# Reordering the transpositions of an attention kernel's output stage

## The reference

```
q, k, v = x @ Wq.T, x @ Wk.T, x @ Wv.T        # 32 heads of 16
q, k    = rope(q), rope(k)
scores  = q k^T / 4 + banded learned bias, causal
attn    = softmax(scores, with a learned offset per head in the denominator) @ v
x1 = layernorm(x + attn @ Wo.T)
y  = mxfp4(x1) @ mxfp4(W).T + b               # blocks of 32 along the row, values rounded to fp4
x2 = layernorm(x1 + y)
```

## Time and profile before

| what | value |
|---|---|
| median of 3 runs | 1728.17 us (1727.54 to 1734.26) |
| the profiled execution's own time | 1727.92 us |
| its span, first to last instruction | 1726.1 us |
| PE busy | 1555.8 us, 90% |
| DVE busy | 1229.9 us, 71% |
| ACT busy | 913.1 us, 53% |
| POOL busy | 194.6 us, 11% |
| mean granted PE clock | 0.952 of full |

### The profile page before, as it was taken

How to read it: one execution, slowest core, us unless ns; L and a number is a source line. 1 busy time by engine, 2 the same in 40 slices (tenths; PEclk the granted TensorE clock), 3 DMA queues, 4 the chain that set the end, 5 groups by cost and what they waited for, 6 DMA issues and landing times.

```text
span 1726.1 us, 59784 instructions
## 1 busy us (share of the span) xinstructions
PE 1555.8 (90%) x22214; PEld 776.2 (45%) x22224; DVE 1229.9 (71%) x3801; ACT 913.1 (53%) x1276; POOL 194.6 (11%) x92
## 2 busy tenths in 40 slices
PE   7999999948998998999899899999999999788773
PEld 3444444412554554555455455455455454344331
DVE  2444444368887888788788788788788884378775
ACT  2333333211665665566566566565566667466764
POOL 4333333240000000000000000000000000023322
PEclk9999999955999999999999999999999999899995
DMA  5444444761343353263264245245244302112211
GB/s 214 148 146 146 158 157 153 137 177 28 79 84 63 70 101 54 59 113 62 53 109 72 53 90 88 56 84 86 63 79 83 70 16 88 37 60 75 73 61 61
DMA packets 127057, 155.70 MB, mean 90 GB/s; under 512 B 18321, under 2 KB 82961, under 8 KB 126514
## 3 DMA queue, kind: packets, MB, share of 16 engines
q1 hardware_dynamic: 126770, 151.86, 37.1%
HBM read 100.52 MB, written 50.50 MB: 87 GB/s over the span
## 4 chain that ended last, share of the span: by engine, by line
PE 60%; DVE 16%; issue 15%; ACT 4%; DMA 2%; POOL 2%; DVEq 1%; SPq 0%; POOLq 0%; ACTq 0%
PE ps L645 14%; PE ps L712 10%; PE ps L671 10%; PE ps L691 10%; PE ps L805 7%; PE ps L697 6%; DVE junk L1152 6%; DVE mx L1145 4%; POOL probs L1024 2%; PE ps L722 1%; DVE mx L1152 1%; ACT probs L947 1%; DMA k_stack<-k_parts 1%; ACT k_stack L937 1%; DMA attn<-wvT 1%
## 5 line engine op out<-in xcount | busy, mean ns | idle before, releaser
L892 ACT ACTIVATE probs<-ps 128x1024 f32<-128x1024 f32 (+3 forms) x768 | 604.2, 812 | 379.9 <-PE ps L697 346.3
L1152 DVE CUSTOM_DVE_ANT_0 junk<-ps,bias_q 128x384 bf16<-128x384 f32 (+2 forms) x1024 | 500.6, 502 | 112.7 <-PE ps L671 92.8
L671 PE MATMUL ps<-k_stack,q_stack 96*32 96x384 bf16 (+3 forms) x6144 | 520.3, 341 | 56.3 <-DVE mx L1152 31.7
L691 PE MATMUL ps<-q_stack,k_stack 99*32 99x512 bf16 (+3 forms) x6144 | 515.1, 333 | 10.0 <-issue 7.7
L1145 DVE TENSOR_REDUCE mx<-ps 128x1 f32<-128x128 f32 (+3 forms) x768 | 362.3, 485 | 34.1 <-PE ps L671 29.3
L697 PE MATMUL ps<-toep,flip 96*32 96x384 bf16 (+2 forms) x5120 | 371.7, 284 | 5.7 <-issue 5.5
L645 PE MATMUL ps<-attn 128*128 128x512 f32 x768 | 332.2, 595 | 10.8 <-DMA attn<-hT 9.6
L712 PE MATMUL ps<-probs,v_sb 128*32 128x512 f32 (+3 forms) x3072 | 318.6, 488 | 0.1
L671 PEld LDWEIGHTS ps<-k_stack,q_stack 96*32 96x32 bf16 x6144 | 169.2, 97 | 297.8 <-DVE mx L1152 106.0
L645 PEld LDWEIGHTS ps<-attn 128*128 128x128 f32 x768 | 146.6, 191 | 195.5 <-issue 195.5
L691 PEld LDWEIGHTS ps<-q_stack,k_stack 99*32 99x32 bf16 x6144 | 167.7, 96 | 137.6 <-issue 68.4
(11 more groups left out here) (98 smaller groups left out, 983.5 us busy)
## 6 DMA issues: line engine op xcount, KB each, us to landing
q_stack<-q_parts SPq DMA_DIRECT2D x192, 128.0 KB, 4.1
k_stack<-k_parts SPq DMA_DIRECT2D x192, 128.0 KB, 4.1
v_dram<-v_sb SPq DMA_DIRECT2D x32, 512.0 KB, 2.7
v_sb<-v_dram SPq DMA_DIRECT2D x128, 128.0 KB, 3.8
q_parts<-q_stack SPq DMA_DIRECT2D x96, 128.0 KB, 1.9
k_parts<-k_stack SPq DMA_DIRECT2D x96, 128.0 KB, 2.0
attn<-hT SPq DMA_DIRECT2D x8, 1024.0 KB, 6.2
q_stack<-h SPq DMA_DIRECT2D x16, 512.0 KB, 4.1
```

The costliest lines, as they stand in the source:

```text
L671: mm = pe.matmul(ps_ring[STRIP * a:STRIP * (a + 1), use.bank, 0:c1 - c0], q_stack[0:STACK, b, hl, i:i + STRIP], k_stack[0:STACK, b, hl, c0 ...
L691: mm = pe.matmul(ps_s[STRIP * a:STRIP * (a + 1), u % 2, hh, 0:w], k_stack[0:ROWS, b, hl, j:j + STRIP], q_stack[0:ROWS, b, hl, i0:i0 + w], ...
L892: act.activation(probs[:, (u // 2) % 3, 2 * pr:2 * pr + 2, 0:w], ps_s[:, pr, :, 0:w], ACT.Exp).then_inc(exp_done, 1)
L1152: ins = dve.tensor_tensor_reduce(out=junk[:, use.bank, 0:c1 - lo], in0=ps_ring[:, use.bank, lo - c0:c1 - c0], in1=bias_q[:, hl, BAND - t0 ...
```

## The change

LEAD becomes 5, the loop bounds are rewritten so that the middle loop still runs twice over four iterations, and PE and ACT get new orders. In iteration i they are now:

- PE: TA(i+5), TQ(i+1), OP(i+4), LI(i+1)
- ACT: CT(i+5), CA(i+6), ROOT0(i+3), NORM0(i+3), CQ(i+1), ROOT1(i), NORM1(i)

DVE, POOL and SP keep their orders; they get one empty iteration (-5) at the start. No instruction is added or taken out, and the waits inside each function are the same.

```
-LEAD = 4
+LEAD = 5
...
-    with eng.Fori(0, (N3 - LEAD) // 4 - 1) as quad:
+    with eng.Fori(0, N3 // 4 - 2) as quad:
...
-    for i in range(N3 - LEAD - 4, N3):
+    for i in range(N3 - 8, N3):
...
             def iteration(at):
-                for work, t in ((transpose_attn, at(4)), (out_projection, at(4)),
-                                (transpose_quantised, at(1)), (linear, at(1))):
+                for work, t in ((transpose_attn, at(5)), (transpose_quantised, at(1)),
+                                (out_projection, at(4)), (linear, at(1))):
...
             def iteration(at):
-                if at(4).exists:
-                    copy_attn_T(at(4).s, at(4).par)
                 if at(5).exists:
-                    copy_attn(at(5).s, at(5).par)
+                    copy_attn_T(at(5).s, at(5).par)
+                if at(6).exists:
+                    copy_attn(at(6).s, at(6).par)
```

## The result

| | before | after |
|---|---|---|
| median | 1729.58 us (1727.54 to 1734.26, 4 runs) | 1814.72 us (1811.39 to 1817.10, 4 runs) |
| profiled execution / its span | 1727.92 / 1726.1 us | 1811.39 / 1809.6 us |
| mean granted PE clock | 0.952 | 0.923 |

The changed kernel is slower by 4.87%: ratio 1.0487, 95% interval 1.0457 to 1.0517. The prediction was 1816 us, within 1785 to 1832. The medians lie 85.1 us apart, where +88.5 was predicted; the fourth run of the kernel before moved its median from 1728.17 to 1729.58 us.

What follows compares the result with a forecast made beforehand. It took a cycle of waits, with no engine full, to set the pace. Start and 12 steps gave +90.2, the drain -1.65, together +88.5 on 1727.92: 1816 us, range 1785 to 1832.

Steps and rivals of the forecast that it cites:

- The closed loop: TQ ahead of OP on PE closes a cycle OP, R1, RD, UN, TQ, OP; OP's 7.13 us no longer cover it.
- Its length: Cycle from OP's start through RD4, UN and TQ: 14.24 + 1.30 + 1.97 + 0.88 = 18.39 us, before OP's clock loss.
- Rival 3: PE's clock stays up over the idle stretch: 17.97 us a step, 1788 us; chance 0.07.
- The deciding branch: RD4 is set by ACT (TA, CT, CA, ROOT0, F0) at S+14.24, 1.86 us after the DVE branch's S+12.38.
- The clock: PE idles some 7 us before TQ, the clock falls to 0.50, and OP loses 1.8 us: step 20.19 us.
- The upper bound: Most that OP could lose to the low clock, taken from stage 2: 2.8 us.
- The number of steps: OP(3) to OP(15) counted as 12 steps of 20.19 us, OP(15) at 1759.9 against 1669.73: +90.2 us.
- The start: OP(0) waits behind TA(1), starting at 1477.5 instead of 1474.56; OP(3) at 1517.6 against 1508.97.
- The drain: After OP(15) the DVE branch decides: 17.45 us to the next TQ against 19.10, -1.65 us; from there 0.
- Rival 1: PE's waits go and nothing replaces them: 12 steps each 2.50 us shorter, -30, 1698 us; chance 0.03.

Runs made afterwards that it cites:

- TQ first alone: Kernel before, LEAD 4 and old ACT order, with only TQ moved ahead of OP on PE: 1813.45 us, ratio 1.0507.
- the clock kept up: Changed kernel with 32 matmuls (28 from step 11 on) that nothing reads in front of each TQ: 1786.35 us, ratio 1.0328.
- the attention half alone: Changed kernel (LEAD 5, earlier copies) with TQ put back behind OP on PE: 1719.64 us, ratio 0.9971 to the kernel before.
- The best order: Changed kernel with PE order OP, TQ, TA, LI and ACT order ROOT0, NORM0, CA, ROOT1, CQ, CT, NORM1: 1698.25 us, ratio 0.9828.

## Why the prediction was right

- *The closed loop.* Right: PE's 7.32 us before TQ are released by POOL, and the run with TQ first alone has the whole loss. PE did not pass over the waiting TQ.
- *Its length.* The sum of instructions and handovers was 18.39 us; with the clock kept up it measured 17.89, against 17.97 predicted for that case. Rival 3's time of 1788 us was met at 1786.35, but not by its books: from TA(0) on that run's profiled execution lost 54.0 us and not the 59.6 of rival 3, mostly because of the number of steps (below), and TA(0) was 6.6 us later than in the kernel before.
- *The deciding branch.* Right: F0 late by 1.73 us where 1.86 was predicted, and moving ROOT0 took it away.
- *The clock.* Right in kind, small in size: I took 1.8 us from two OPs that began low; here the first matmul of LI starts 9.14 us after OP's start (1717.42 to 1726.56, profiled execution of after) where 6.97 is the full-clock distance, so the loss is 2.2. The two OPs that I took it from began 3.1 us after a TA that had itself begun low; here only TQ, 0.83 us, stands ahead. Whether that makes the difference is not shown. The upper bound has a small slip: in the windows the clock rose at 426.9 and not 426.7, which makes it 2.9 instead of 2.8. The full step is 20.46 us (OP(3) to OP(13): 204.58 / 10) instead of 20.19.
- *The number of steps.* Here the working was wrong, and by luck it made up for the clock. I counted 12 full steps. The step into OP(14) has no CA any more and took 19.53 us; the one into OP(15) has no TA and took 17.42. That is -3.4 us, against +2.7 from ten steps of 0.27 more. Without this slip the forecast would have been some 3 us lower, inside its range all the same.
- *The start.* OP(0) started 5.75 us after TA(0), 5.99 predicted; OP(3) +8.68, +8.6 predicted. The close hit is in part luck: OP(0) lost 1.7 us to the clock instead of 1.2, and from TA(4) to OP(3) it took 9.79 us instead of 10.2.
- *The drain.* -0.98 instead of -1.65, by a larger clock loss in OP(15) (9.60 us instead of the 8.9 taken).
- *Rival 1*, 2.50 us less a step, failed where the prediction said, at the time of `a_ready`. In the attention half alone only 0.42 us a step of it came. The best order, which opens two more waits, gains 2.26 us a step and is then held by DVE's work.

## What to carry to other kernels

Before moving an instruction ahead of a long one on an in-order engine, ask what the wait of the moved one depends on: if that leads back, through any engines, to the long one's earlier turn, the long one no longer hides it and the step becomes the sum round the loop. A wait that is taken away in a software pipeline uncovers the next loop, often only a few tenths shorter; write the loops down with their lengths, and move the work (here ROOT1 ahead of CQ) that is on the longest. Count separately the last steps of a pipeline, in which some works have run out.

## What the runs showed of the hardware

With 24 additional matmuls PE sat idle for 2.13 us between full work in almost every step. In every second of them the granted clock then fell to 0.50, about 1 us after work had begun again, and OP behind it lost 1.7 us; in the others it stayed at 1.00, so the length of the idle stretch alone does not decide. Idle stretches of 0.41 us (32 additional matmuls) and the waits of 1.12 and 1.38 us in each step of the kernel before left it at 1.00. I had expected a fall only after the long waits. What OP loses after a fall also differs: with steps of 20.46 us it settled at 2.2 us, with steps of 17.55 to 18.95 us it went round 1.0, 2.5 and 1.5. Why is not shown.
